# Quantising the feed-forward's weights inside the second attention's loop instead of in the quantised attention's preparation

## The chip, the cores and the metric

The kernel is one program on one core of a Trainium2 chip. Its time is the device time of one execution in microseconds. The five engines run their own instruction streams and meet at semaphores: TensorE (PE, with its weight loads as PEld), VectorE (DVE), ScalarE (ACT), GpSimd (POOL) and SyncE (SP), whose queue issues nearly all DMAs.

## What is computed

A decoder of four layers over 16 tiles of 128 tokens with 256 features. Each layer adds a gated attention and a gated feed-forward to `x`:

```python
x = x + tanh(g_xattn[1]) * L1_xattn(layernorm(x), ctx)      # the second attention, 32 heads of 8
x = x + tanh(g_ffn[1])   * L1_ffn(layernorm(x))             # sparse mixture of experts
x = x + tanh(g_xattn[2]) * L2_xattn(layernorm(x), ctx)      # the quantised attention, 16 heads of 16
x = x + tanh(g_ffn[2])   * L2_ffn(layernorm(x))             # the quantised feed-forward
```

The change is about the weights of the last of these. They are quantised to integers of 4 bits, which depends on nothing but the weights themselves:

```python
def weight_scale(W):
    return max(abs(W)) / 7
sw1 = weight_scale(W1)                        # W1: 1024 x 256
W1_q = clip(round(W1 / sw1), -8, 7) * sw1
b1_q = clip(round(b1 / (s1 * sw1)), INT32_MIN, INT32_MAX) * (s1 * sw1)
# the same for W2 (256 x 1024), b2 and s2
```

## The kernel before

The program is a row of stages with a barrier between them. Three are named here. The order of the instructions on each engine is written out by hand, and every dependence is a semaphore that the code waits for.

**The second attention, `rms_attention`.** After projections (a block of its own) it has a loop over the 16 tiles `t`, 797 to 911 us in the profile. GpSimd prepares the queries and keys of a tile in `stacks(t)` (six or so short instructions, L1080 to L1088) and the values in `values_staged(t)` (L1091); it runs one tile ahead. TensorE transposes the queries (`queries_turned`, `rms_TT<-rms_qs`) and the keys (`keys_turned`, `rms_TT<-rms_ks`), multiplies them (`scores`, L1287), multiplies with the values (`values`, L1301) and turns the result back (`turned_back`, L1311). ScalarE copies the queries and takes the exponentials. VectorE has, for each tile, `output(t - 1, 1)`, `evacuate(t, 0)` (L1374), `keys(t + 1)` (L1367, the copy `rms_kT`), `output(t, 0)`, `evacuate(t, 1)` and the statistics for the next layer (L1391). SyncE issues nothing in this loop.

**The quantised attention's preparation, in `quantised_attention`,** 1265 to 1372 us: SyncE loads the context, the attention's weights, and last, in `next_weights.load`, the feed-forward's weights as float32 (`qf_f`, 1 MB each), its biases and scales. Then come the projection of keys (`keys(p)`, pairs of tiles), values with the transposes of the normalised rows (`rows_turned`, and `low(p)` on VectorE, L2317), the values' integers (`value_integers`, L2348 to L2355), the transposes of keys, values and queries (`qa_TR`), and the projection of queries (`queries(p)`). The main loop over 256 pairs of tile and head follows.

**Class `QuantisedWeights`** quantises the feed-forward's weights within that preparation. Its VectorE steps stand between the `low(p)` and between the `queries(p)`: `magnitudes` (greatest absolute value of each partition, L1963), `scales` (seven instructions on two columns, L1968 to L1976), `divided` (L1993), `integers` (L1997), `hidden_bias` (four instructions on 8 columns) and `output_bias` (three on 256 columns). `greatest` is one GpSimd instruction, which takes the maximum over the partitions:

```python
    def greatest(self, pool):
        pool.wait_ge(self.s_am, 2)
        self.nc.gpsimd.partition_all_reduce(self.amx[:, :], self.am[:, :], P, bass.bass_isa.ReduceOp.max).then_inc(self.s_amx, 1)
```

It stands between the last `key_halves` and the 16 additions of `qa_bp` to `X` (L2131). `chained` gives an instruction a semaphore and makes VectorE wait for it before the next.

Of the kernel before, what the change touches and what calls it, by code (L numbers as in the profile page):

```python
# [7 lines left out]
F32 = mybir.dt.float32  # L8
# [1038 lines left out]
def rms_attention(nc, sh, ctxT, weights, gate, clear):  # L1047
# [13 lines left out]
    with ExitStack() as ctx:  # L1061
# [188 lines left out]
        ROUNDS = NB * NR  # L1250

        with nc.Block() as block:
            @block.gpsimd
            def _(pool):
                for t in range(2, NB):
                    pool.wait_ge(s_TK, t - 1)
                    stacks(pool, t)
                    pool.wait_ge(s_O, 2 * (t - 1))
                    values_staged(t)
# [102 lines left out]
            def _(dve):  # L1362
# [33 lines left out]

                keys(0)
                for t in range(NB):
# [9 lines left out]
                    if t:  # L1408
                        next_statistics(t - 1)
                output(NB - 1, 1)  # L1410
# [502 lines left out]
class QuantisedWeights:  # L1913


    F, NF = 1024, 8

    def __init__(self, nc, ctx, a):
        self.nc, self.a = nc, a

        def sb(n, shape, dt=F32):
            return ctx.enter_context(nc.sbuf_tensor("qf_" + n, shape, dt))

        self.w1 = sb("w1", [P, KT * self.F], F16)
        self.w2 = sb("w2", [P, self.NF * D], F16)
        self.b1 = sb("b1", [P, self.NF])
        self.b2 = sb("b2", [P, D])
        self.sa = sb("sa", [P, 2])
        self.rsa = sb("rsa", [P, 2])
        self.c = sb("c", [P, 8])  # L1930

    def prepare(self, ctx):
        nc = self.nc

        def sb(n, shape, dt=F32):
            return ctx.enter_context(nc.sbuf_tensor("qf_" + n, shape, dt))

        self.f1 = sb("f1", [P, KT * self.F])
        self.f2 = sb("f2", [P, self.NF * D])
        self.am, self.amx, self.sw, self.rsw = (sb(x, [P, 2]) for x in ("am", "amx", "sw", "rsw"))  # L1940
        self.s_load, self.s_am, self.s_amx, self.s_c, self.s_w = (
            nc.alloc_semaphore(name="qf_" + n) for n in ("load", "am", "amx", "wchain", "weights"))

    def load(self, sp):
        a = self.a
        sp.dma_start(self.f1[:, :], a["qf_w1"]).then_inc(self.s_load, 16)
        sp.dma_start(self.f2[:, :], a["qf_w2"]).then_inc(self.s_load, 16)
        sp.dma_start(self.b1[:, :], a["qf_b1"]).then_inc(self.s_load, 16)
        sp.dma_start(self.b2[:, :], a["qf_b2"].partition_broadcast(P)).then_inc(self.s_load, 16)
# [7 lines left out]
    def start(self, dve):  # L1957
        self.chained = chain_on(dve, self.s_c)

# [1668 lines left out]
```

## Time and profile before

| | |
|---|---|
| median of 3 runs | 2326.14 us (2323.9 to 2328.3) |
| the profiled execution | 2327.31 us, span 2325.6 us |
| PE busy | 1923.0 us, 83% |
| DVE busy | 1656.2 us, 71% |
| ACT busy | 1343.0 us, 58% |
| POOL busy | 896.6 us, 39% |
| granted TensorE clock, mean | 0.798 of full speed |

The shares are means over stages with different limits, so they don't say what a change in one stage is worth. For that the stage's own instructions are read in order of time: which instruction had to wait, and who released it. The clock in the profile's windows is a share of full speed: 1.00 is 2.4 GHz and 0.50 is 1.2 GHz.

### The profile page before, as it was taken

What the parts mean: (1) busy time and instruction counts of PE and PEld (TensorE: products, weight loads), DVE (VectorE), ACT (ScalarE), POOL (GpSimd) and SP (SyncE); (2) the same over time, 40 slices, a digit from 0 to 9 for tenths busy, and PEclk for the clock granted to TensorE, in tenths of its full rate; (3) what the DMA queues carried; (4) which work ended last, traced back from release to release, by engine and by line L of the source; (5) the groups of instructions that cost most, each with busy time, mean ns of one, the idle gap of its engine ahead of it and who ended that gap; (6) DMA issues with size and microseconds to landing.
All of it is one profiled execution on the core that took longest, in us unless ns stands there. A gap on an engine that the chain in (4) does not pass through costs nothing. (4 is left out here: it accounts for less than half of the span.)

```text
span 2325.6 us, 49109 instructions
## 1 busy us (share of the span) xinstructions
PE 1923.0 (83%) x17689; PEld 1096.0 (47%) x17713; DVE 1656.2 (71%) x2772; ACT 1343.0 (58%) x1831; POOL 896.6 (39%) x779
## 2 busy tenths in 40 slices
PE   3875999999997786799997868888888888468855
PEld 1343656656564465478874433333333333334523
DVE  4776765555555566853336989999999999467975
ACT  3444643333334676543333459999999999445565
POOL 4750000000001462600024438888888888423301
PEclk8776999999998898999998765555555555588989
DMA  7334212122122303522223016666665667120100
GB/s 209 87 124 170 68 65 69 67 66 68 63 67 86 105 3 117 222 49 69 65 64 107 34 28 111 113 112 112 110 113 111 113 110 112 25 73 2 21 20 28
DMA packets 384868, 195.32 MB, mean 84 GB/s; under 512 B 312301, under 2 KB 355311, under 8 KB 382703
## 3 DMA queue, kind: packets, MB, share of 16 engines
q1 hardware_dynamic: 381617, 184.47, 32.8%
q0 software_dynamic: 3072, 8.39, 1.1%
q8 instruction: 120, 1.97, 0.4%
q14 instruction: 59, 0.48, 0.1%
HBM read 94.99 MB, written 23.09 MB: 51 GB/s over the span
## 5 line engine op out<-in xcount | busy, mean ns | idle before, releaser
L2470 POOL CAST qa_pT<-qa_eT 128x2048 bf16<-128x2048 uint8 x256 | 478.0, 1896 | 109.9 <-PE qa_OY L2496 94.4
L2583 ACT ACTIVATE qa_e<-qa_scores,qa_nb 128x2048 uint8<-128x2048 f32 x256 | 510.4, 1994 | 4.2
L2593 DVE TENSOR_SCALAR_CACHE_REDUCE qa_scores<-qa_S,qa_sq 128x1024 f32<-128x1024 f32 (+1 forms) x256 | 456.0, 1830 | 4.2 <-PE qa_S L2488 3.3
L2488 PE MATMUL qa_S<-qa_kT,qa_qT 32*128 32x512 f16 x1024 | 373.2, 615 | 95.6 <-DVE qa_scores L2593 94.2
L1118 POOL MEMSET rms_nothing<- 128x512 f16 x1 | 0.5, 525 | 580.2 <-POOLq L3517 580.2
L2488 PEld LDWEIGHTS qa_S<-qa_kT,qa_qT 32*128 32x128 f16 x1024 | 64.8, 108 | 310.1 <-DVE qa_scores L2593 266.9
L975 PE MATMUL moe_G<-hT,moe_W 128*128 (+1 forms) x792 | 193.8, 381 | 7.0 <-DVE moe_zero L943 7.0
L984 PE MATMUL moe_O<-moe_W,moe_ap 128*128 (+1 forms) x1584 | 194.5, 273 | 4.1 <-DVE moe_ap L939 4.1
L915 ACT ACTIVATE moe_ap<-moe_a 128x512 f16<-128x512 f32 x132 | 83.0, 629 | 193.2 <-DVE moe_a L937 193.2
L975 PE MATMUL moe_U<-hT,moe_W 128*128 (+1 forms) x792 | 193.0, 380 | 0.0
L984 PEld LDWEIGHTS moe_O<-moe_W,moe_ap 128*128 128x128 f16 x1584 | 154.7, 98 | 50.4 <-DVE moe_ap L939 3.9
L2593 DVE TENSOR_SCALAR_CACHE_REDUCE qa_scores<-qa_S,qa_sq,qa_first_mx 128x1024 f32<-128x1024 f32 x128 | 174.4, 1363 | 0.0
L2496 PEld LDWEIGHTS qa_OY<-qa_V,qa_pT 128*128 128x128 bf16 x4096 | 119.1, 104 | 111.0 <-POOL qa_pT L2470 68.1
L934 DVE TENSOR_TENSOR moe_t<-moe_sg,moe_wb 128x512 f32<-128x512 f32 x132 | 91.4, 692 | 112.1 <-ACT moe_sg L910 107.6
L939 DVE TENSOR_TENSOR moe_ap<-moe_a,moe_ap 128x512 f16<-128x512 f32 x132 | 91.5, 693 | 91.7 <-ACT moe_ap L915 91.7
L910 ACT ACTIVATE moe_sg<-moe_G 128x512 f32<-128x512 f32 x132 | 78.8, 597 | 132.9 <-PE moe_G L975 132.7
L2496 PE MATMUL qa_OY<-qa_V,qa_pT 128*128 128x16 bf16 x4096 | 130.7, 175 | 6.9 <-ACT qa_y L2568 4.1
L1807 PE MATMUL moe_GU<-moe_xs,moe_W 128*128 128x256 f16 x1104 | 129.5, 274 | 3.9 <-issue 3.9
L1723 DVE TENSOR_TENSOR moe_a<-moe_GU,moe_sg 128x512 f32<-128x512 f32 x78 | 53.8, 689 | 99.6 <-PE moe_GU L1807 87.6
L975 PEld LDWEIGHTS moe_U<-hT,moe_W 128*128 (+1 forms) x792 | 77.7, 98 | 94.1 <-issue 1.1
L1603 ACT ACTIVATE moe_ap<-moe_a 128x512 f16<-128x512 f32 x78 | 49.2, 630 | 119.1 <-DVE moe_a L1723 119.1
L1556 POOL DMA_INDIRECT H<-moe_ys_rows,moe_slot x32 | 31.5, 985 | 223.1 <-DMA moe_ys_rows<-moe_ys 213.6
(436 smaller groups left out, 3533.4 us busy)
## 6 DMA issues: line engine op xcount, KB each, us to landing
moe_wb<-weights_T SPq DMA_DIRECT2D x264, 128.0 KB, 2.8
moe_W<-in_moe_w SPq DMA_DIRECT2D x40, 384.0 KB, 11.5
moe_W<-in_moe_w SPq DMA_DIRECT2D x11, 1152.0 KB, 17.2
moe_xs_rows<-rms_nothing SPq DMA_DIRECT2D x46, 128.0 KB, 1.9
moe_ys_rows<-moe_ys SPq DMA_DIRECT2D x23, 256.0 KB, 2.1
conv_rows<-conv_parts SPq DMA_DIRECT2D x16, 256.0 KB, 3.2
qa_eT<-qa_e SPq DMA_TRANSPOSE x256, 3.1
conv_qst<-conv_rows SPq DMA_DIRECT2D x96, 32.0 KB
```

The source lines that it names most:

```text
L910: nc.scalar.activation(sg[:, u, :], G[:, u, :], ACT.Silu).then_inc(s_sg[u], 1)
L915: nc.scalar.activation(ap[:, u, 0, :], a[:, u, :], ACT.Copy).then_inc(s_hi[u], 1)
L934: nc.vector.tensor_tensor(t1[:, u, :], sg[:, u, :], wb[:, u, :], ALU.mult).then_inc(s_t1[u], 1)
L939: nc.vector.tensor_tensor(ap[:, u, 1, :], a[:, u, :], ap[:, u, 0, :], ALU.subtract).then_inc(s_lo[u], 1)
L975: last = nc.tensor.matmul(X_[:, u, :], sh.W[:, f, wp, base + k * P:base + (k + 1) * P], sh.hT[:, xp, k, bass.ds(c * CT, CT)], start=i == 0 ...
L984: last = nc.tensor.matmul(O[:, t, :], ap[:, u, xp, t * P:(t + 1) * P], sh.W[:, f, wp, 4 * P:TW], start=False, stop=False, skip_group_check ...
L1807: last = nc.tensor.matmul(out[:, half * SLOT_TILE:(half + 1) * SLOT_TILE], W[:, bass.ds(f, 1), wp, base + k * P:base + (k + 1) * P], xs[:, ...
L2470: nc.gpsimd.tensor_copy(pT[:, u % RING, :, :].rearrange("p (b r) q -> p b r q", r=2), pairs).then_inc(s_cast, 1)
L2488: last = nc.tensor.matmul(S[:, banks[i], :], qT[rows, g, t * P:(t + 1) * P], kT[rows, g, parts[i] * QW:(parts[i] + 1) * QW], start=True, s ...
L2496: last = nc.tensor.matmul(O[:, h * HD:(h + 1) * HD], pT[:, u % RING, b, :], V[:, b, h * HD:(h + 1) * HD], start=b == 0, stop=b == NB - 1)
L2583: nc.scalar.activation(e8[:, u % RING, :], scores[:, u % RING, :], ACT.Exp, bias=nb[:, p % 2, i:i + 1], accum_out=sums[:, u:u + 1]).then_i ...
L2593: nc.vector.tensor_scalar(target, S[:, banks[0]:banks[-1] + 1, :], sq[:, t, h:h + 1], so_far, ALU.mult, ALU.max, accum_out=greatest).then_ ...
```

## The change

All work on the feed-forward's weights and biases moves from the quantised attention's preparation into the second attention's loop. The float32 weights are loaded when the loop starts, VectorE quantises them in nine places at the end of an iteration, SyncE stores the results in DRAM, and the preparation only loads them from there (0.5 MB each, float16, and 274 columns of constants). The arithmetic is the same. New are a memset of the constants, which the loads wait for, three stores and their waits on SyncE's queue, and the three loads.

```diff
-def rms_attention(nc, sh, ctxT, weights, gate, clear):
+def rms_attention(nc, sh, ctxT, weights, gate, clear, staged, staged_gate):
...
+        staged.prepare(ctx)
 
         with nc.Block() as block:
+            @block.sync
+            def _(sp):
+                staged.load(sp)
+                staged.store(sp)
+
             @block.gpsimd
             def _(pool):
                 for t in range(2, NB):
+                    if t == 7:
+                        staged.greatest(pool)
                     pool.wait_ge(s_TK, t - 1)
                     stacks(pool, t)
                     pool.wait_ge(s_O, 2 * (t - 1))
                     values_staged(t)
...
+                staged.start(dve)
                 keys(0)
                 for t in range(NB):
...
                     if t:
                         next_statistics(t - 1)
+                    if t in (2, 3):
+                        staged.magnitudes(dve, t - 2)
+                    if t == 7:
+                        staged.scales(dve, staged_gate)
+                    if t in (8, 10):
+                        staged.divided(dve, (t - 8) // 2)
+                    if t in (9, 11):
+                        staged.integers(dve, (t - 9) // 2)
+                    if t == 12:
+                        staged.hidden_bias(dve)
+                    if t == 13:
+                        staged.output_bias(dve)
...
     def load(self, sp):
         a = self.a
+        sp.wait_ge(self.s_c, 1)
         sp.dma_start(self.f1[:, :], a["qf_w1"]).then_inc(self.s_load, 16)
...
+    def store(self, sp):
+        sp.wait_ge(self.s_w, 1)
+        sp.dma_start(self.home1, self.q1[:, :]).then_inc(self.s_home, 16)
+        sp.wait_ge(self.s_w, 2)
+        sp.dma_start(self.home2, self.q2[:, :]).then_inc(self.s_home, 16)
+        sp.wait_ge(self.s_b, 1)
+        sp.dma_start(self.home_constants, self.constants[:, :]).then_inc(self.s_home, 16)
+        sp.wait_ge(self.s_home, 48)
...
     def start(self, dve):
         self.chained = chain_on(dve, self.s_c)
+        self.chained(self.nc.vector.memset(self.constants[:, :], 0.0))
...
+    def load(self, sp):
+        sp.dma_start(self.w1[:, :], self.staged.home1).then_inc(self.s_load, 16)
+        sp.dma_start(self.w2[:, :], self.staged.home2).then_inc(self.s_load, 16)
+        sp.dma_start(self.constants[:, :], self.staged.home_constants).then_inc(self.s_load, 16)
+        sp.wait_ge(self.s_load, 48)
...
                     for p in range(PAIRS):
                         key_halves(p)
-                    next_weights.greatest(pool)
                     pool.wait_ge(s_norm, NB)
...
-                    next_weights.start(dve)
                     low(0)
-                    next_weights.magnitudes(dve, 0)
                     low(1)
-                    next_weights.magnitudes(dve, 1)
                     low(2)
...
                     low(3)
-                    next_weights.scales(dve, next_gate)
                     low(4)
-                    next_weights.divided(dve, 0)
                     low(5)
-                    next_weights.integers(dve, 0)
-                    next_weights.hidden_bias(dve)
                     low(6)
-                    next_weights.output_bias(dve)
                     low(7)
                     value_integers()
...
                     for p in range(PAIRS):
                         queries(p)
-                        if p == 3:
-                            next_weights.divided(dve, 1)
-                        if p == 5:
-                            next_weights.integers(dve, 1)
```

Three places show what the built program makes of it. First GpSimd's instructions in the second attention's loop, between tiles 6 and 7 (`rms_vx` ends tile 6, `rms_qkv` starts the stacks of tile 7). Before:

```order
L1087 TENSOR_TENSOR rms_qs<-rms_qkv,rms_qs 128x32x8
L1088 TENSOR_TENSOR rms_ks<-rms_qkv,rms_ks 128x32x8
L1091 COPY rms_vx<-rms_qkv 128x32x8
L1080 TENSOR_TENSOR rms_qkv<-rms_qkv,rms_rs 128x512
L1084 CAST rms_qs<-rms_qkv 128x32x8 x2
```

and now:

```order
L1087 TENSOR_TENSOR rms_qs<-rms_qkv,rms_qs 128x32x8
L1088 TENSOR_TENSOR rms_ks<-rms_qkv,rms_ks 128x32x8
L1091 COPY rms_vx<-rms_qkv 128x32x8
L1988 ISA
L1988 ISA staged_amx<-staged_am 128x2
L1080 ISA
L1080 TENSOR_TENSOR rms_qkv<-rms_qkv,rms_rs 128x512
L1084 CAST rms_qs<-rms_qkv 128x32x8 x2
```

The maximum over the partitions (`staged_amx`) comes with one unnamed instruction ahead of it and one behind it, which the builder adds; they stood around it in the preparation too (as `MODIFY_POOL_CONFIG` in the profile), and now all three stand ahead of tile 7's stacks.

Second VectorE's instructions at the end of iteration 7 of that loop, as they are now; the seven rows with `staged` are new, and each iteration from 8 to 13 has its own insertion in the same place:

```order
L1382 COPY rms_oT<-rms_O 128x512
L1403 BN_AGGR row_mv<-row_stats 128x2
L1399 BN_STATS row_stats<-X 128x6
L2002 RECIPROCAL staged_constants<-staged_sa 128x2
L2004 TENSOR_SCALAR staged_sw<-staged_amx 128x2
L2005 RECIPROCAL staged_rsw<-staged_sw 128x2
L2007 TENSOR_TENSOR staged_constants<-staged_sa,staged_sw 128x2
L2008 RECIPROCAL staged_constants<-staged_constants 128x2
L2009 TENSOR_TENSOR staged_constants<-staged_constants 128x1
L2010 TENSOR_TENSOR staged_constants<-staged_constants,gates 128x1
L1388 RECIPROCAL rms_inv<-rms_B 128x16
```

The insertion is behind the last statistics of an iteration and ahead of the first `output` of the next one, which has `evacuate` and the copy of the keys behind it.

Third VectorE's instructions in the quantised attention's preparation between two `low` steps (`hT<-qa_hT_TP`), before:

```order
L2317 TENSOR_TENSOR hT<-qa_hT_TP,hT 128x2x256
L1963 TENSOR_REDUCE qf_am<-qf_f 128x1
L2317 TENSOR_TENSOR hT<-qa_hT_TP,hT 128x2x256
L1963 TENSOR_REDUCE qf_am<-qf_f 128x1
L2317 TENSOR_TENSOR hT<-qa_hT_TP,hT 128x2x256
L2368 TENSOR_SCALAR qa_bp<-qa_bp,gates 128x256
```

and now:

```order
L2374 TENSOR_TENSOR hT<-qa_hT_TP,hT 128x2x256 x3
L2422 TENSOR_SCALAR qa_bp<-qa_bp,gates 128x256
L2374 TENSOR_TENSOR hT<-qa_hT_TP,hT 128x2x256 x5
```

The `low` steps stand next to each other, with only the scaling of `qa_bp` left among them.

## Rows read from the trace of the kernel before

**Rows 1.** windows by stage: span, each engine's busy us (instructions), PEclk, DMA share, GB/s

```profile
797.00:911.00 114.00, 93.30 (x1918) 69.42 (x1916) 67.22 (x176) 78.24 (x82) 59.15 (x113) 0.96 0.01 2
...
1265.00:1372.00 107.00, 80.01 (x501) 44.46 (x502) 81.50 (x136) 47.75 (x77) 50.52 (x51) 0.73 0.15 52
```

**Rows 2.** timeline, VectorE in the loop: start, us, instruction, [idle before <-releaser]

```profile
823.81 0.40 DVE L1391 BATCH_NORM_STATS2 row_stats<-X 128x6 f32<-128x256 f32 x1
824.56 0.26 DVE L1380 RECIPROCAL rms_inv<-rms_B 128x16 f32<-128x16 f32 x1 [0.35 <-PE rms_B L1311]
...
825.92 0.69 DVE L1374 COPY rms_oT<-rms_O 128x512 f32<-128x512 f32 x1 [0.40 <-PE rms_O L1301]
826.53 0.68 DVE L1367 COPY rms_kT<-rms_TT 128x1024 f16<-128x1024 f16 x1
```

**Rows 3.** timeline, TensorE in the loop, one tile apart

```profile
820.73 0.40 PE L1287 MATMUL rms_S<-rms_qT,rms_kT 32*128 32x128 f16 x8 [0.86 <-DVE rms_kT L1367]
...
823.31 0.62 PE L1265 MATMUL rms_TT<-identh,rms_qs 128*128 128x128 f16 x8
...
827.27 0.40 PE L1287 MATMUL rms_S<-rms_qT,rms_kT 32*128 32x128 f16 x8 [0.86 <-DVE rms_kT L1367]
```

**Rows 4.** timeline, GpSimd in the loop

```profile
820.30 0.67 POOL L1088 TENSOR_TENSOR rms_ks<-rms_qkv,rms_ks 128x256 f16<-128x256 f32 x1
823.14 0.40 POOL L1091 COPY rms_vx<-rms_qkv 128x256 f32<-128x256 f32 x1 [2.18 <-PE rms_O L1301]
823.50 1.08 POOL L1080 TENSOR_TENSOR rms_qkv<-rms_qkv,rms_rs 128x512 f32<-128x512 f32 x1
```

**Rows 5.** timeline, GpSimd in the quantised attention's preparation

```profile
1320.36 0.37 POOL L1955 PARTITION_ALL_REDUCE qf_amx<-qf_am  x1 [5.84 <-DVE qa_bp L2368]
1327.63 15.19 POOL L2131 TENSOR_TENSOR X<-X,qa_bp 128x256 f32<-128x256 f32 x16 [6.90 <-issue]
```

**Rows 6.** instructions of lines L1955 and L2131 on GpSimd's queue

```profile
L1955 POOLq MODIFY_POOL_CONFIG  x2: 15/15/15, 1314.5 to 1314.5; - x2
...
L2131 POOLq MODIFY_POOL_CONFIG  x2: 82/82/83, 1320.7 to 1320.7; - x2
```

**Rows 7.** windows at the loop's start and inside it, columns as in Rows 1

```profile
795.90:806.10 10.20, 6.50 (x88) 4.77 (x88) 0.93 (x2) 6.45 (x7) 3.81 (x7) 0.50 0.01 2
...
815.00:880.00 65.00, 56.40 (x1199) 42.22 (x1198) 41.77 (x109) 47.58 (x50) 42.24 (x80) 1.00 0.01 3
```

**Rows 8.** timeline, TensorE, 32 value products at either clock

```profile
804.33 1.89 PE L1301 MATMUL rms_O<-rms_E,rms_vx 128*32 128x128 f32 x32
...
808.88 1.08 PE L1301 MATMUL rms_O<-rms_E,rms_vx 128*32 128x128 f32 x32
```

**Rows 9.** VectorE on `qf_f` alone, then on `qf_b` alone; and `scales`, one line

```profile
1313.00:1330.00 17.00, 7.04 (x4) 1.00 0.01 1
1355.00:1364.00 9.00, 2.50 (x2) 1.00 0.01 2
...
1313.00:1330.00 17.00, 2.73 (x7) 1.00 0.01 1
...
L1970 DVE TENSOR_SCALAR qf_sw<-qf_amx 128x2 f32<-128x2 f32 x1 | 0.2, 170 | 0.5 <-POOL qf_amx L1955 0.5
```

**Rows 10.** instructions of line L2323: min/median/max ns

```profile
L2323 DVE TENSOR_SCALAR qa_sk<-qa_sk x8: 181/730/3712, 1280.2 to 1309.1; 128x32 f32<-128x32 f32 x8
```

**Rows 11.** timeline, TensorE in the preparation, its waits

```profile
1319.58 0.63 PE L2182 MATMUL qa_hT_TP<-ident,H 128*128 128x128 f32 x4 [0.87 <-DVE hT L2317]
...
1340.84 0.62 PE L2204 MATMUL qa_TR<-identh,qa_ints 128*128 128x128 f16 x8 [2.59 <-DVE qa_ints L2355]
...
1369.12 0.97 PE L2188 MATMUL qa_TR<-identh,qa_stack 128*128 128x128 f16 x8 [2.17 <-POOL qa_stack L2134]
```

**Rows 12.** timeline, ScalarE in the preparation

```profile
1330.22 9.65 ACT L2267 ACTIVATE qa_kT<-qa_TR 128x512 f16<-128x512 f16 x16 [4.04 <-PE qa_TR L2188]
```

**Rows 13.** DMA issues: count, KB each, median us to landing

```profile
qf_f<-in_qf_w SPq DMA_DIRECT2D x2, 1024.0 KB, 8.8
```

More of the change, by code:

```diff
@@ L1910, in tensor, with __init__, dram @@
                 last.then_inc(self.s_T, 1)
-class QuantisedWeights:
+class StagedWeights:
     F, NF = 1024, 8
-    def __init__(self, nc, ctx, a):
+    CONSTANTS = 8 + D + 8 + 2
+    def __init__(self, nc, a):
         self.nc, self.a = nc, a
[L1921 to L1930, printed above, removed]
+        def dram(n, width, dt):
+            return nc.dram_tensor("qf_home_" + n, [P, width], dt, kind="Internal").ap()
+        self.home1, self.home2 = dram("w1", KT * self.F, F16), dram("w2", self.NF * D, F16)
+        self.home_constants = dram("constants", self.CONSTANTS, F32)
     def prepare(self, ctx):
@@ L1988, in output_bias @@
         chained(nc.vector.tensor_scalar(b[:, :], b[:, :], MAGIC, 2.0 ** 31 - 1, ALU.subtract, ALU.min))
-        chained(nc.vector.tensor_scalar(b[:, :], b[:, :], -2.0 ** 31, None, ALU.max))
+        nc.vector.tensor_scalar(b[:, :], b[:, :], -2.0 ** 31, None, ALU.max).then_inc(self.s_b, 1)
     def divided(self, dve, i):
@@ L1995, in integers, with __init__, sb, quantised_attention @@
     def integers(self, dve, i):
-        f, w = (self.f1, self.f2)[i], (self.w1, self.w2)[i]
+        f, w = (self.f1, self.f2)[i], (self.q1, self.q2)[i]
         self.nc.vector.tensor_scalar(w[:, :], f[:, :], MAGIC, None, ALU.subtract).then_inc(self.s_w, 1)
-def quantised_attention(nc, sh, a, gate, next_weights, next_gate):
+class QuantisedWeights:
+    F, NF = StagedWeights.F, StagedWeights.NF
+    def __init__(self, nc, ctx, staged):
+        self.nc, self.staged = nc, staged
+        def sb(n, shape, dt=F32):
+            return ctx.enter_context(nc.sbuf_tensor("qf_" + n, shape, dt))
+        self.w1 = sb("w1", [P, KT * self.F], F16)
+        self.w2 = sb("w2", [P, self.NF * D], F16)
+        self.constants = sb("constants", [P, staged.CONSTANTS])
+        self.b1, self.b2 = self.constants[:, 0:8], self.constants[:, 8:8 + D]
+        self.c, self.rsa = self.constants[:, 8 + D:16 + D], self.constants[:, 16 + D:18 + D]
+        self.s_load = nc.alloc_semaphore(name="qf_load")
+    def load(self, sp):
[3 more added lines that the diff above has]
+        sp.wait_ge(self.s_load, 48)
+def quantised_attention(nc, sh, a, gate, next_weights):
     NH, HD = 16, 16
@@ L2041, in quantised_attention @@
             rsv = sb("rsv", [P, KT], F32, inner)
-            next_weights.prepare(inner)
             vT = cf
@@ L3539, in program @@
             mixture(MOE0, 0)
+        staged = StagedWeights(nc, a)
         with own_semaphores(nc):
-            rms_attention(nc, sh, a["ctxT"], {"q": a["rms_wq"], "kv": a["rms_wkv"]}, sh.gates[:, 2:3], xs_rows)
+            rms_attention(nc, sh, a["ctxT"], {"q": a["rms_wq"], "kv": a["rms_wkv"]}, sh.gates[:, 2:3], xs_rows, staged, sh.gates[:, 5:6])
         with own_semaphores(nc):
@@ L3544, in program @@
         with own_semaphores(nc):
-            quantised = QuantisedWeights(nc, ctx, a)
-            quantised_attention(nc, sh, a, sh.gates[:, 4:5], quantised, sh.gates[:, 5:6])
+            quantised = QuantisedWeights(nc, ctx, staged)
+            quantised_attention(nc, sh, a, sh.gates[:, 4:5], quantised)
         with own_semaphores(nc):
```

16 lines of the change are left out of this document (11 added, 5 removed).

## Prediction

> **What bounds the kernel now.** I read first the windows by stage [rows 1], for how busy each engine is in the two stages that the change touches; then the timeline of each engine in them, for who waits for whom. In the second attention's loop no engine is full: of the 114 us TensorE is busy 93, ScalarE 78, VectorE 67, GpSimd 59. It is a ring that takes 6.54 us a tile (820.73 to 827.27 for the same instruction [rows 3]). In each turn TensorE stops once, for 0.86 us, for VectorE's copy of the turned keys `rms_kT` [rows 3]. That copy starts the moment `evacuate` ends (825.92, then 826.53), and in front of it VectorE was idle only twice in that part of the turn: 0.35 us before `output(t, 1)` and 0.40 us before `evacuate` [rows 2]. So VectorE has 0.75 us to spare at the place of the insertions, and no more; its mean idle share (41%) lies elsewhere in the turn. GpSimd ends its stacks at 820.97 (820.30 + 0.67 [rows 4]), and TensorE takes them at 823.31 [rows 3]: 2.34 us to spare.
>
> In the preparation VectorE looks full (81.5 of 107 us [rows 1]), and the moved work seems to be what fills it. But other engines run close behind, as the gain below shows.
>
> **What the preparation gives back.** Removed from VectorE are 7.04 us on `qf_f` and 2.73 us on the biases between 1313 and 1330, 2.50 us between 1355 and 1364, and seven small instructions of some 0.2 us [rows 9]: 7.04 + 2.73 + 2.50 + 1.4 = 13.7 us. Of this little comes back.
> - First part. Without it `value_integers` starts about 3.9 us earlier (the `low` steps then follow ScalarE's copies), its product `qa_ints` too. TensorE waits for `qa_ints` at 1340.84 [rows 11]. But it also needs TensorE's key transposes copied out, and ScalarE does that in 16 copies back to back from 1330.22 to 1339.87 [rows 12]. So 0.97 us is free at once. TensorE's one stop for a `low` step, 0.87 us at 1319.58 [rows 11], goes as well and starts those copies by that much or a little more earlier: together 1.9 us.
> - Second part. The two `qf_f` instructions among the queries, 2.50 us, push VectorE's last queries back. TensorE, with its own projections and transposes, takes 2.6 us a pair there against VectorE's 2.4, an estimate from following the queries through the trace, so VectorE can't be ahead of it by all of that: 1.5 us comes back at the end, where TensorE waits 2.17 us (1369.12 [rows 11]).
>
> Sum: -3.4 us. The bounds are -1.9 (the first part alone) and -7 (TensorE's clock, half from about 1342 to 1352, stays full). The loads there shrink from 2 MB to 1.1 MB and were last on the queue anyway: nothing. GpSimd's additions of `qa_bp` start earlier; nobody waits for them.
>
> **What the loop pays for GpSimd.** The maximum over the partitions itself takes 0.37 us [rows 5]. On either side of it stands a `MODIFY_POOL_CONFIG`. From the first, at 1314.5 [rows 6], to the maximum at 1320.36, GpSimd is idle for 5.84 us; from the second, at 1320.7 [rows 6], to its next instruction at 1327.63 it is idle for 6.90 us [rows 5], and the profile names no one that it waits for there. Part of the first interval is a wait for VectorE: the second `magnitudes` was ready at about 1318.8. So the first switch costs between 1.5 and 5.84 us; as the second is 6.90 with nothing to wait for, I take 5.84 as a full switch. In the preparation both were covered, since nobody needed GpSimd. In the loop all three stand directly behind `rms_vx`, where GpSimd goes on without a pause (823.14 + 0.40, then 823.50 [rows 4]); its idle 2.18 us is ahead of `rms_vx` and covers nothing. Tile 7's stacks are 5.84 + 0.37 + 6.90 = 13.1 us late, and behind them wait `queries_turned(7)` on TensorE, which blocks everything after it there, then ScalarE and VectorE. Less the 2.34 to spare: **+10.8 us**. Bounds: 8.8 - 2.3 = 6.5 with the short first switch, 11.8 with two at 6.90.
>
> The Trainium skill (GPSIMD Engine Reference, 2.1 Instruction dispatch) says that the first call of a freshly loaded kernel pays about 6 us, measured as the gap from the configuration to that call less the wait. Taken so, two switches give 5.95 x 2 + 0.37 - 2.34 = 9.9 us, an estimate by that page; our first interval less its wait is 1.5 us, so here loading and waiting overlapped, and only the second agrees.
>
> **The clock behind that stop.** After the pause before the loop, TensorE's granted clock was 0.50 from 795.9 to 806.1 and 1.00 after [rows 7]; TensorE restarted at about 796.6. A pause of 11 us should do the same. At half clock 32 value products take 1.89 us against 1.08 [rows 8], 1.75 times. TensorE's 5.67 us a tile (56.40 / 65 x 6.54 [rows 7]) would be 9.9 if all of it stretched so, and about 9 if two thirds do; in the 9.5 us at half clock that is about one tile, **+3.2 us**. Bounds 0 (no drop) and 4.3.
>
> **What the loop pays for VectorE.** Nine insertions, t = 2, 3 and 7 to 13. The same instructions took 13.7 us. Each has 0.75 us to spare and passes the rest on: `rms_kT` is later by it, TensorE stands still, and the ring has no slack in which to catch up. 13.7 - 9 x 0.75 = 6.9 us. The largest are the two reductions, 2.2 us each, so 1.45 each.
>
> Besides, the insertion starts at 824.21, when GpSimd's `rms_qkv` runs to 824.58 [rows 2, 4]. A VectorE instruction on SBUF alone that meets GpSimd can be held: L2323, on 32 columns, took 181 ns at best, 730 in the median and 3712 once, when GpSimd had three instructions in a row [rows 10]. With 0.37 us for each of the seven insertions that have a `TENSOR_SCALAR`: +2.6 us. **+9.5 us** together. Bounds: 6.9 without any wait; if each of the seven waits to the end of GpSimd's stacks, at 827.5, it is 7 x 3.3 = 23 instead of 2.6, so 30.
>
> The Trainium skill (SBUF — State Buffer, Who interferes with whom) has GpSimd and VectorE lock each other out of a shared pair of ports, whole instructions long, with `tensor_scalar` among those that take it and `tensor_reduce` never. By that rule the two reductions pay nothing extra and the others 0.37 us or more, which is what the sum has; the trace shows the holding, not whether a lock is handed over in the short gaps of the stacks.
>
> **Hidden.** The loads, 1 MB in 8.8 us [rows 13], are issued before the first keys and needed at t = 2, more than 20 us later. The memset falls in VectorE's wait before the first key copy. The stores (0.5 MB twice) start behind t = 9, 11 and 13, and the last, of 0.14 MB, has two tiles, 13 us, until the block's end; if that cover were gone it would be some 3 us. Nothing else is on SyncE's queue in the loop.
>
> **Sum.** -3.4 + 10.8 + 3.2 + 9.5 = +20.1 us. The profiled execution took 2327.31 us with its span of 2325.6, so 1.7 us lies around the span, and it is 1.2 us above the median of 2326.1. Neither changes with the edit: the profiled one would be 2347.4, the median 2346.2. I predict **2346 us, slower by 0.86%**.
>
> **Rivals.**
> - *The insertions are free*: VectorE is idle 41% of the loop, and TensorE might catch up. Then -3.4 + 10.8 + 3.2 gives 2337. Against it: the 0.86 us for `rms_kT` in each turn. Chance 0.11.
> - *The first switch is short or overlaps*, the 1.5 us of its lower bound: 4.3 less, 2342. For it speaks that the maximum began 1.5 us after its input. 0.13.
> - *Port waits run long*: VectorE is held through two or three of GpSimd's instructions per insertion, some 1.9 us instead of 0.37, so +10: 2356. For it the one wait of 3.7 us, against it the median. 0.13.
> - *The switch costs nothing in the loop* (the other side): if GpSimd's idle time around the maximum was something of the preparation and not of the switch, the stop at t = 7 is 0.37 us and hidden, and the clock does not drop. Place: GpSimd between `rms_vx` of tile 6 and the stacks of tile 7; price: the 14.0 us of both terms. With insertions at their 6.9 us that is -3.4 + 6.9, 2330, within 0.2% of before. It decides when the stop is under 2.34 us plus about one. Against it the 6.90 us with nothing to wait for. 0.06, and 0.02 for an actual gain through more from the preparation.
> - *As forecast*: 0.55, with its own range 2340 to 2353.
>
> **How the numbers follow.** Where this kernel's measurement can tell a change from none is about 0.2%, 4.7 us: faster is below 2321.4, slower above 2330.8. All but the fourth rival are slower: faster 0.02, same 0.06, slower 0.92. The range 2335 to 2358 takes in the free insertions at the bottom and the long port waits at the top; it leaves out the fourth rival and the far ends, less than 2 in 10.
>
> **What would show it.** In the loop: GpSimd idle for 5 to 7 us on either side of the maximum; TensorE waiting some 11 us for the stacks of tile 7 with the clock at 0.50 after it; `rms_kT` waits of 0.86 us grown to about 2.3 at two tiles and to 1.3 to 2 at seven more; the stage from 797 to 911 longer by 23 to 24 us. In the preparation: `qa_ints` ahead of ScalarE's last key copy, the stage 3 to 4 us shorter. The prediction is wrong if the stop of GpSimd is below 6 us, if `rms_kT` is not late, or if insertions wait for GpSimd's whole burst.

## The result, and the profile after

The changed kernel takes 2346.1 us in the median of six runs, against 2325.0 us in six runs of the kernel before, measured beside it. The ratio is 1.0083, with a 95% interval of 1.0064 to 1.0101, so the change makes the kernel slower by 15 to 23 us.

The two profiled executions alone would mislead: their spans are 2325.6 and 2332.9 us, 7.3 us apart, and the changed kernel's, of 2334.6 us, is 11.5 us below its median. The stages tell why. Windows by stage of the changed kernel (span, busy us and instructions of PE, PEld, DVE, ACT, POOL, then PEclk, DMA share, GB/s): all before the loop, the loop from the first `rms_TT` to the mixture's first instruction, the projection of keys, values with `rows_turned`, and the transposes and queries:

```profile
0.00:790.30 790.30, 679.29 (x5081) 400.09 (x5082) 474.34 (x783) 323.44 (x519) 126.08 (x88) 0.94 0.29 97
790.30:928.20 137.90, 100.17 (x1920) 74.55 (x1920) 81.35 (x198) 78.63 (x82) 62.85 (x115) 0.88 0.07 27
...
1283.40:1318.70 35.30, 24.14 (x129) 11.86 (x130) 22.02 (x47) 12.05 (x20) 23.25 (x22) 0.66 0.38 128
1318.70:1338.10 19.40, 18.35 (x115) 10.82 (x113) 13.20 (x20) 12.96 (x24) 14.16 (x20) 1.00 0.00 1
1338.10:1379.20 41.10, 31.80 (x258) 21.19 (x256) 27.07 (x50) 22.87 (x33) 6.51 (x10) 0.72 0.00 1
```

The same windows of the kernel before, by its own landmarks:

```profile
0.00:796.60 796.60, 687.30 (x5080) 402.63 (x5081) 475.22 (x782) 323.75 (x519) 126.22 (x88) 0.92 0.30 96
...
796.60:911.20 114.60, 93.69 (x1920) 69.82 (x1920) 67.33 (x177) 78.44 (x82) 59.35 (x114) 0.96 0.01 2
1266.20:1308.20 42.00, 30.73 (x129) 13.87 (x130) 27.47 (x50) 12.05 (x20) 24.16 (x22) 0.51 0.38 132
1308.20:1329.60 21.40, 20.07 (x114) 11.28 (x113) 19.63 (x34) 12.97 (x24) 5.88 (x8) 0.93 0.00 1
1329.60:1371.50 41.90, 28.71 (x261) 19.08 (x260) 34.35 (x53) 22.70 (x33) 20.46 (x22) 0.85 0.00 1
```

The loop is longer by 23.3 us, 137.9 against 114.6. Two stages with the same TensorE instructions are shorter: all before the loop by 6.3 us (granted clock 0.94 against 0.92) and the projection of keys by 6.7 us (0.66 against 0.51). The last two stages are 2.0 and 0.8 us shorter. Whether the 6.7 us belongs to the change is the first question for the experiments.

In the loop, the timeline of GpSimd shows the maximum with its two switches, which answers to [rows 5]:

```profile
834.07 0.40 POOL L1091 COPY rms_vx<-rms_qkv 128x256 f32<-128x256 f32 x1 [3.82 <-PE rms_O L1309]
840.05 0.38 POOL L1988 PARTITION_ALL_REDUCE staged_amx<-staged_am  x1 [5.58 <-issue]
847.24 1.06 POOL L1080 TENSOR_TENSOR rms_qkv<-rms_qkv,rms_rs 128x512 f32<-128x512 f32 x1 [6.82 <-issue]
```

GpSimd is idle 5.58 us ahead of the maximum, with its input ready since tile 3, and 6.82 us behind it. TensorE in the same place, against [rows 3]:

```profile
822.49 0.40 PE L1295 MATMUL rms_S<-rms_qT,rms_kT 32*128 32x128 f16 x8 [2.43 <-DVE rms_kT L1375]
...
831.65 0.40 PE L1295 MATMUL rms_S<-rms_qT,rms_kT 32*128 32x128 f16 x8 [2.12 <-DVE rms_kT L1375]
...
838.20 0.40 PE L1295 MATMUL rms_S<-rms_qT,rms_kT 32*128 32x128 f16 x8 [0.86 <-DVE rms_kT L1375]
...
851.24 1.03 PE L1273 MATMUL rms_TT<-identh,rms_qs 128*128 128x128 f16 x8 [10.39 <-POOL rms_ks L1088]
...
857.28 0.60 PE L1295 MATMUL rms_S<-rms_qT,rms_kT 32*128 32x128 f16 x8 [0.79 <-DVE rms_kT L1375]
...
888.15 0.40 PE L1295 MATMUL rms_S<-rms_qT,rms_kT 32*128 32x128 f16 x8 [1.59 <-DVE rms_kT L1375]
```

TensorE waits 10.39 us for the stacks of tile 7. Its 0.86 us for `rms_kT` grew to 2.43 and 2.12 behind the two reductions and to 1.59 behind an integer step. The reader can take the loop apart by the distance of one tile's first scores to the next, which is 6.54 us in [rows 3], and 6.54 or 6.55 us in every turn of the kernel before but the first. What exceeds 6.54 is: 1.58 and 2.62 us behind the reductions of t = 2 and 3, 12.54 and, in the next turn, 1.66 around the stop, 0.95 behind `scales`, 1.37, 0.73, 0.73 and 0.74 behind the four big steps, 0.42 behind `hidden_bias`, nothing behind `output_bias`. Their sum is 23.3, the whole growth of the loop. (In the turn behind the first big step the excess is 1.37 and the wait 0.86: a drop of the clock, below, took the place of the wait.)

Three of these have a part that the waits don't show. Windows of TensorE (busy us, PEclk):

```profile
823.50:826.90 3.40, 3.40 (x54) 0.50 0.00 0
...
844.00:861.00 17.00, 8.98 (x112) 0.50 0.00 1
...
874.70:878.10 3.40, 3.40 (x46) 0.50 0.00 0
```

The clock is at half (1.2 GHz) from 844, inside the stop, until 861, 9.8 us after TensorE restarts; that is the 3.8 us in the two steps around the stop beyond the wait of 10.39. And it falls to half for 3.4 us twice more, at 823.5 and 874.7, where TensorE had only waited for late key copies. These two drops make 2.62 and 1.37 of what would be 1.58 and 0.73.

### The profile page after: what moved, and what is told of

Same layout as the page of the kernel before. It is cut to its first block and busy times, and to the rows that moved or that the text cites. A ratio compares the mean times of both kernels' runs of the same rounds, so it can differ in the third digit from the quotient of the medians.

```text
span 2332.9 us, 49118 instructions
## 1 busy us (share of the span) xinstructions
PE 1914.2 (82%) x17689; PEld 1097.0 (47%) x17713; DVE 1650.0 (71%) x2773; ACT 1343.0 (58%) x1831; POOL 892.6 (38%) x779
## 5 line engine op out<-in xcount | busy, mean ns | idle before, releaser
L1828 PEld LDWEIGHTS moe_GU<-moe_xs,moe_W 128*128 x1104 | 108.8, 99 | 17.5 <-issue 4.2
```

What stands on the lines that cost most here:

```text
L1828: last = nc.tensor.matmul(out[:, half * SLOT_TILE:(half + 1) * SLOT_TILE], W[:, bass.ds(f, 1), wp, base + k * P:base + (k + 1) * P], xs[:, ...
```

## The experiments

### The changed kernel once more

No edit.

> The changed kernel once more, unaltered, for a second profile. Forecast: the same terms, so 2344 to 2348 us, 20 us over the kernel before; loop stage 137 to 138 us (first rms_TT to the first instruction of the mixture), with the stop of 10 to 11 us for GpSimd and TensorE at half clock behind it. One question is open here: in the first profile of the changed kernel the projection of keys in the quantised attention took 35.3 us where it took 42.0 before, with 24 us at half clock instead of 44. If the change causes that (ScalarE, VectorE or the queue act otherwise there), it comes again, 35 us; if it is chance of the execution, this profile can show anything from 35 to 42.

Measured: 2347.9 us, ratio 1.0111 (1.0081 to 1.0141), which overlaps with the first interval. Windows of this profile, the loop and the preparation's three stages:

```profile
791.50:928.20 136.70, 98.54 (x1920) 73.70 (x1920) 81.30 (x198) 78.54 (x82) 62.87 (x115) 0.90 0.08 27
1283.10:1325.10 42.00, 30.74 (x129) 13.74 (x130) 27.45 (x50) 12.08 (x20) 24.16 (x22) 0.51 0.32 107
1325.10:1345.30 20.20, 20.06 (x114) 11.34 (x113) 12.61 (x17) 12.75 (x24) 13.09 (x19) 0.93 0.00 1
1345.30:1383.80 38.50, 27.95 (x258) 18.84 (x255) 27.05 (x50) 22.56 (x33) 6.72 (x11) 0.85 0.00 1
```

The projection of keys takes 42.0 us at clock 0.51, as before the change. So the 6.7 us were chance of one execution, and the question is settled by the same program. At the clock of the kernel before (0.93 and 0.85 in the last two stages of both) these stages are 1.2 and 3.4 us shorter: the preparation gives back 4.6 us here, and 2.8 us in the first profile, whose last stage ran at 0.72. The stop was 10.36 us again (TensorE restarts at 853.17), but the clock behind it came back 3.9 us after the restart and not 9.8:

```profile
847.20:857.10 9.90, 3.93 (x52) 0.50 0.01 2
```

The step around the stop exceeds 6.54 by 12.05 us and the next one by nothing, so the clock cost 1.7 us and not 3.8. Two short drops of the clock came here as well, behind the second reduction and behind the first big step.

### The maximum through DRAM instead of GpSimd

```diff
-                    if t == 7:
-                        staged.greatest(pool)
...
+    def turn(self, sp):
+        sp.wait_ge(self.s_am, 2)
+        sp.dma_start(self.am_home, self.am[:, :]).then_inc(self.s_amd, 16)
+        sp.wait_ge(self.s_amd, 16)
+        sp.dma_start(self.amb[:, :, :], self.am_home.rearrange("p i -> (p i)").partition_broadcast(P)).then_inc(self.s_amb, 16)
...
+        chained(nc.vector.tensor_reduce(out=self.amx[:, :], in_=self.amb[:, :, :].rearrange("p q i -> p i q"), axis=AXX, op=ALU.max))
```

> The changed kernel with the maximum over partitions taken without GpSimd: SyncE stores the 128x2 maxima in DRAM and loads them back to every partition, VectorE reduces 128x2x128 at the head of the scales of tile 7. No switch on GpSimd; all else, insertions too, as in the changed kernel. Theory (switch 10.8 to 10.4 of stop and 3.2 to 3.8 of clock): 14 us less than the changed kernel, about 2332, less 0.4 us for the longer scales; loop stage 124. Rival 'the switch costs nothing, the insertions do it all': no change, 2346. Rival 'insertions are free': 2346 - 20 = 2326 or so. The round trip of the maxima has four tiles, 26 us, and should be hidden; if it is not, the wait is at the scales of tile 7.

Measured: 2332.0 us, ratio 1.0028 (1.0013 to 1.0044), loop 125.2 us. Windows of the loop and of the preparation's last two stages together; then SyncE's queue at the round trip:

```profile
793.00:918.20 125.20, 96.86 (x1920) 72.14 (x1920) 82.03 (x199) 78.55 (x82) 62.67 (x114) 0.92 0.10 31
1315.40:1375.40 60.00, 49.16 (x370) 30.26 (x368) 39.64 (x66) 35.64 (x57) 19.82 (x28) 0.87 0.00 1
```

```profile
831.35 0.33 SPq L1990 DMA_DIRECT2D staged_am_home<-staged_am  x1
834.27 0.33 SPq L1992 DMA_DIRECT2D staged_amb<-staged_am_home  x1
```

The store is done after 2.9 us (the second transfer is issued then), and nobody waits for the round trip. Its price is VectorE's reduction of 0.42 us at the head of `scales`: that turn exceeds 6.54 by 1.59 us instead of 0.95. Without GpSimd's part the loop is 12.7 and 11.5 us shorter than in the two profiles of the changed kernel, and 10.6 us longer than before; 2.0 us of that are two short drops of the clock to half. Both rivals fall: the switch costs, and the insertions cost.

### The switch alone, in the kernel before

```diff
+                nc.gpsimd.memset(spare[:, :], 1.0).then_inc(s_spare, 1)
+                pool.wait_ge(s_spare, 1)
                 for t in range(2, NB):
+                    if t == 7:
+                        nc.gpsimd.partition_all_reduce(spare[:, 2:4], spare[:, 0:2], P, bass.bass_isa.ReduceOp.max).then_inc(s_spare, 1)
```

> The kernel before, with one addition: GpSimd takes an idle maximum over partitions of a 128x2 tile of ones ahead of the stacks of tile 7 in the second attention's loop; nobody reads it. Nothing of the quantisation is moved. Theory: both switches and their clock fall on the path, 10.4 to 10.8 + 3.2 to 3.8 = 13.6 to 14.6 us more than before, about 2340. Rival 'the switch costs nothing in the loop': 2326. Rival 'first switch short when nothing is waited for' (1.5 us): 2335.

Measured: 2337.3 us, ratio 1.0066 (1.0043 to 1.0089), loop 127.0 us, +12.4. GpSimd and TensorE in its timeline:

```profile
838.57 0.37 POOL L1261 PARTITION_ALL_REDUCE rms_spare<-rms_spare  x1 [5.78 <-issue]
845.80 1.06 POOL L1080 TENSOR_TENSOR rms_qkv<-rms_qkv,rms_rs 128x512 f32<-128x512 f32 x1 [6.86 <-issue]
```

```profile
836.52 0.40 PE L1293 MATMUL rms_S<-rms_qT,rms_kT 32*128 32x128 f16 x8 [0.86 <-DVE rms_kT L1373]
849.79 1.03 PE L1271 MATMUL rms_TT<-identh,rms_qs 128*128 128x128 f16 x8 [10.63 <-POOL rms_ks L1088]
855.33 0.40 PE L1293 MATMUL rms_S<-rms_qT,rms_kT 32*128 32x128 f16 x8 [0.87 <-DVE rms_kT L1373]
```

With none of VectorE's insertions in the loop and an input that was ready before tile 2, the first switch is 5.78 us. That rules out the rival of a short first switch (1.5 us). The stop is 10.63 us; the step from 836.52 to 855.33 is 18.81, that is 12.27 over 6.54, so the clock costs 1.6 us; it came back 3.8 us after TensorE's restart. The total, +15 us (10 to 21), agrees with this but is less sharp. The two single parts add up in the loop: 12.4 us for the switch and 10.6 us for the insertions are 23.0, against 23.3 and 22.1 for both in one kernel.

### No quantisation at all

Three memsets ahead of the first key copy fill what is stored in the homes; the loads, GpSimd's `greatest` and VectorE's nine insertions are left out, so the last feed-forward computes with empty weights:

```diff
-                staged.load(sp)
                 staged.store(sp)
...
-                    if t in (2, 3):
-                        staged.magnitudes(dve, t - 2)
...
-                    if t == 13:
-                        staged.output_bias(dve)
```

> The changed kernel without the quantisation: no loads of the float32 weights, no VectorE or GpSimd work on them; the homes in DRAM are filled with zeros and ones from three memsets before the loop, so the last feed-forward computes with empty weights (that part of the computation is left out). It measures what the preparation alone gives back. Theory: loop as before, 114.6 us; preparation -3.4 us by the forecast (bounds -1.9 and -7), total about 2322.7. If the shorter projection of keys of the changed kernel's profile (-6.7 us) is caused by the change and not by chance, total about 2316.

Measured: 2322.0 us, ratio 1.0000 (0.998 to 1.0021).

```profile
791.90:906.60 114.70, 93.75 (x1920) 69.88 (x1920) 69.32 (x180) 78.45 (x82) 59.26 (x114) 0.96 0.04 13
1301.90:1359.60 57.70, 47.01 (x373) 30.27 (x373) 40.17 (x68) 35.59 (x57) 19.81 (x28) 0.87 0.00 1
```

The loop is that of before, and values, transposes and queries take 57.7 us where the kernel before has 21.4 + 41.9 = 63.3, 5.6 us less at about the same clock (0.93 and 0.85 before, 0.87 here). The interval of the total reaches from -4.6 to +4.9 us and so just holds a gain of 4; it shows that the time taken away, 13.7 us of VectorE, isn't given back, and rules out the 9.5 us by which the first profile's preparation seemed shorter.

### TensorE kept busy through the stop

```diff
                 def queries_turned(t):
+                    if t == 7:
+                        pe.wait_ge(s_kT, t)
+                        for i in range(160):
+                            nc.tensor.transpose(TT[:, i % NG, :], sh.identh[:, :], sh.identh[:, :])
                     pe.wait_ge(s_lo, t + 1)
-                    if t:
+                    if t and t != 7:
                         pe.wait_ge(s_kT, t)
```

> The changed kernel with 160 idle transposes of the identity into the free rms_TT on TensorE ahead of its wait for the stacks of tile 7, so that TensorE stays busy through GpSimd's stop. The stop itself remains. Theory: the half clock behind the stop (from 844 to 861 us in the changed kernel) is due to TensorE's pause; without the pause the steps behind it are at full clock and the kernel is 3.8 us faster than the changed one, 2342. Rival 'the half clock there has another cause, or costs nothing': 2346.

Measured: 2340.3 us, ratio 1.0073 (1.0052 to 1.0094), loop 136.4 us. TensorE in its timeline, then two windows, through the stop and behind it:

```profile
841.48 9.11 PE L1280 MATMUL rms_TT<-identh 128*128 128x128 f16 x160
852.09 0.62 PE L1273 MATMUL rms_TT<-identh,rms_qs 128*128 128x128 f16 x8 [1.51 <-POOL rms_ks L1088]
```

```profile
841.50:850.60 9.10, 9.09 (x162) 1.00 0.01 2
850.60:867.70 17.10, 13.89 (x296) 1.00 0.01 3
```

The clock stays at 1.00 and the step around the stop exceeds 6.54 by 10.47 us, against 14.20 (in two steps), 12.05 and 12.27 without filling. So the half clock behind the stop is due to TensorE's pause and costs 1.6 to 3.7 us: the mechanism is shown, and the gain of 3.8 us that I expected is the top of it. The loop won only 0.3 to 1.5 us, because three dips of the clock to half, of 3.4 us each, fell elsewhere in it (two in the changed kernel). The total, 0.1% under the changed kernel's first ratio and 0.4% under its second, doesn't tell 1.6 from 3.8.

### The insertions at another place

The kernel with the maximum through DRAM; the nine `if t ...` lines stand ahead of `output(t, 0)`:

```diff
                     if t + 1 < NB:
                         keys(t + 1)
+                    if t in (2, 3):
+                        staged.magnitudes(dve, t - 2)
...
+                    if t == 13:
+                        staged.output_bias(dve)
                     output(t, 0)
                     evacuate(t, 1)
```

> The kernel with the maxima through DRAM, with its nine insertions whole as they were, but at another place of the iteration: behind the copy of the turned keys and ahead of output(t, 0), where VectorE is idle for 1.08 us, and further on for 0.39, 0.35 and 0.40 us before the next key copy. Theory (only what VectorE has to spare ahead of the next key copy counts): 2.2 us to spare there instead of 0.75, so that of the insertions (2.27 us twice, 1.54 us four times, 2.0, 1.4 and 0.9 us) next to nothing passes on; loop 115 to 116 us, total about 2320 to 2322, 10 us less than with the maxima through DRAM and the old places. Rival 'TensorE waits for output(t, 0) or evacuate(t, 1) instead': what exceeds 1.08 us passes on, 1.19 x 2 + 0.46 x 4 + 0.9 + 0.3 = 5.4 us, loop 120, total 2326.

Measured: 2332.1 us against 2337.2 for the kernel before, measured beside it (on another chip than the runs above: a stage that no edit touches, the mixture, takes 368 us there instead of 355), ratio 0.999 (0.9974 to 1.0007). Window of the loop; VectorE at t = 2; TensorE in the two turns with the reductions:

```profile
791.10:907.10 116.00, 93.89 (x1920) 69.82 (x1920) 80.78 (x199) 78.42 (x82) 59.57 (x114) 0.96 0.10 33
```

```profile
814.59 0.68 DVE L1374 COPY rms_kT<-rms_TT 128x1024 f16<-128x1024 f16 x1
815.19 2.28 DVE L2001 TENSOR_REDUCE staged_am<-staged_f 128x1 f32<-128x2048 f32 x1
...
819.69 0.26 DVE L1387 RECIPROCAL rms_inv<-rms_B 128x16 f32<-128x16 f32 x1 [0.35 <-PE rms_B L1318]
```

```profile
819.00 0.66 PE L1318 MATMUL rms_B<-ident,rms_oT 128*128 128x128 f32 x4 [0.47 <-DVE rms_oT L1381]
```

The loop is 116.0 us instead of 125.2. At t = 2 the reduction takes 2.28 us, and VectorE has caught up when it waits 0.35 us again before `output(t, 1)`, so the next key copy is on time. The theory holds for `rms_kT`. The rival holds in small: at the two reductions TensorE stops 0.47 us for `rms_oT`, and these turns exceed 6.54 by 0.54 each; with 0.18 once more the insertions cost 1.3 us, where the old places cost 10.2 (8.2 of waits and the 2.0 of the clock).

### VectorE's work in pieces

Again without GpSimd's maximum. The reductions are cut to 512 columns, `divided` and `integers` to 1024, `scales` and the biases to one or two instructions, and `piece(t, 0)` stands behind `keys(t + 1)`, `piece(t, 1)` at the end of the iteration:

```diff
                         keys(t + 1)
+                    staged.piece(t, 0)
                     output(t, 0)
...
+                    staged.piece(t, 1)
...
+        self.pieces = {(1, 1): greatest_of(0), (2, 0): greatest_of(1), (2, 1): greatest_of(2), (3, 0): greatest_of(3),
...
+                       (8, 0): div(0, 0), (9, 0): div(0, 1), (10, 0): whole(0, 0), (11, 0): whole(0, 1),
```

> As the kernel with the maxima through DRAM, and VectorE's work cut to fit its idle time: reductions of 512 columns, divisions and integers of 1024 columns, scales and biases two instructions at a time, in two places of each iteration from tile 1 to 15: behind the copy of the turned keys (1.08 us idle there) and at the end (0.75 us). The same work, with more and shorter instructions. Theory (ring with 0.75 and 1.08 us to spare, port waits about 0.26 us each): next to nothing passes on, loop 115 to 117 us, so the preparation's gain remains: 2322 to 2325, that is 0 to 0.2% faster than before. Rival 'each VectorE instruction among GpSimd's pays the port': 27 pieces x 0.3 us or more = 8 us, 2331.

> The kernel with VectorE's work in pieces once more, unaltered, since its first interval (0.9962 to 1.0003) does not tell it from the kernel before. Theory: loop 115.0 and the preparation 3.4 to 4.6 us shorter, 0.15 to 0.2% faster than before; the stages from the first qa_VP to the first qa_S take 58.7 us at 10 us of half clock.

Measured: 2321.2 us against 2322.3, ratio 0.9983 (0.9962 to 1.0003); again, on the other chip, 2334.1 against 2337.2, 0.9995 (0.9979 to 1.001). The window of the loop in the first profile (115.4 us in the second), then one of VectorE's groups there:

```profile
799.40:914.40 115.00, 93.69 (x1920) 69.88 (x1920) 83.19 (x211) 78.46 (x82) 59.49 (x114) 0.96 0.11 33
```

```profile
L2026 DVE TENSOR_SCALAR staged_f<-staged_f,staged_rsw 128x1024 f32<-128x1024 f32 x4 | 3.7, 917 | 0.0
```

VectorE is busy 83 us of the loop instead of 67, and all turns are 6.54 or 6.55 us but the first, as before, and one of 6.74 (6.75 in the second profile). So 16 us more work in the loop cost 0.2 us in the turns, and 0.4 us in the loop as a whole: the rival of 8 us for the ports falls, since what VectorE waits for GpSimd there (0.74 to 1.00 us for one and the same kind of piece) is covered too. Neither interval tells this version from the kernel before, and the same is so of the insertions behind the key copy. By the stages it should be 4 us faster (0.4 us more in the loop, some 4.6 less in the preparation), 0.2% or about what can be measured; that it beats the kernel before is not shown.

### The kernel before once more

> The kernel before once more, unaltered, for a second profile and as a measure of the method: ratio 1.000. The projection of keys took 25.9 to 32.6 us in seven profiles with the same instructions; here it can be any of these. The stages from the first qa_VP to the first qa_S should take 63 us again (63.3 and 62.9 in the two profiles with the quantisation in the preparation, 57.6 to 60.5 in the six without).

Measured: 2339.2 against 2337.2 us, ratio 1.000 (0.9978 to 1.0022). Windows of the loop and of the preparation's last two stages, and the latter for the pieces, measured beside it:

```profile
793.60:908.60 115.00, 94.15 (x1920) 70.13 (x1920) 67.38 (x178) 78.48 (x82) 59.25 (x114) 0.95 0.01 2
1319.10:1384.80 65.70, 53.00 (x369) 32.25 (x368) 53.93 (x86) 35.92 (x57) 26.25 (x29) 0.79 0.00 1
```

```profile
1318.10:1380.30 62.20, 51.47 (x370) 32.32 (x368) 40.27 (x69) 35.83 (x57) 20.71 (x29) 0.81 0.00 1
```

The clock in these stages differs from one execution to the next whichever the kernel is, here 0.79. I expected 63 us and it took 65.7. The projection of keys, counted as in the expectation, from its own first matmul, took 32.6 us, the upper end of what was seen.

## Why the prediction was right

Forecast 2346 us and +20.1; measured 2346.1, and +19.3 by the ratio (15 to 23). The mechanisms were right; that the sum came out so near is in part luck, since two terms were off and an effect that was not forecast made up for it:

| term | forecast | measured |
|---|---|---|
| preparation gives back | -3.4 | -4.6 (mean of eight profiles less mean of three) |
| GpSimd's stop | +10.8 | +10.4, +10.4, +10.6 |
| the clock behind it | +3.2 | +3.8, +1.7, +1.6; gone when TensorE was kept busy |
| VectorE's insertions | +9.5 | +7.5, and 1.7 and 2.1 more for short dips of the clock |
| loop as a whole | +23.5 | +23.3, +22.1 |

**What bounds the loop.** Right: a ring without slack. What delays `rms_kT` beyond what VectorE has to spare ahead of it is never caught up, as every turn of 6.54 us behind a long one shows. It was shown from both sides: the same nine insertions cost 10.2 us with 0.75 us to spare and 1.3 us with 2.2 us to spare, and the same work in pieces 0.2 us.

**GpSimd's stop.** Right, in size and in the mechanism. The first switch was the open part, 1.5 to 5.84 us by [rows 5]; it is 5.50 to 5.78 us in the loop with its input long ready, and the second 6.82 to 7.14. The estimate of 9.9 us from the first-call figure of the Trainium skill (GPSIMD Engine Reference, 2.1 Instruction dispatch), taken for both switches, was as near as mine: 5.58 + 0.38 + 6.82 less the 2.34 to spare are 10.4, so 5.95 us are too much for the first switch and too little for the second. The 1.5 us in the preparation fit loading that overlaps with a wait: the time from the configuration to the maximum is nearly the same with a wait in it (5.84) and without (5.50 to 5.78).

**The clock behind the stop.** The mechanism is right, and keeping TensorE busy showed it. The size is that of one execution: half clock lasted 9.8 us after TensorE's restart in the first profile, 3.9 us in the second and 3.8 us with the switch alone, and 3.8, 1.7 and 1.6 us were paid. The forecast took 9.5 us at half clock from [rows 7] as if that were fixed. (In its working, two thirds of 5.67 us stretched 1.75 times give 8.5 us a tile and not 9; the 3.2 us come out with 8.5, as 9.5 / 8.5 x 2.8.)

**The insertions.** Their term, 9.5 us, was mis-sized: without the clock they cost 7.5. The two reductions passed on 1.58 each (forecast 1.45), the four big steps 0.73 each (forecast 0.5 and 0.37 for the port), `scales` 0.95 (1.0), and the two biases 0.42 and nothing, where the forecast had 2.0 for both. So `rms_kT` was late at five tiles behind the reductions and not at seven: nothing was left of the insertion at t = 13, and a drop of the clock hid that at t = 8. Two things were wrong with the port waits. The big steps took 1.54 us instead of 1.28 and 1.22, so 0.26 and 0.32 us each and not 0.37. And the 2.73 us of the biases held port waits already: two instructions took 0.83 and 0.70 us in the preparation, where GpSimd's additions had just begun (1327.63 in [rows 5]), and 0.29 each in the loop, where all seven took 2.13. This is the first of the two, in the kernel before:

```profile
L1988 DVE TENSOR_SCALAR qf_b<-qf_b 128x256 f32<-128x256 f32 x1 | 0.8, 829 | 0.0
```

This is the row of `divided` in the changed kernel, against 1.28 in the preparation before:

```profile
L2027 DVE TENSOR_SCALAR staged_f<-staged_f,staged_rsw 128x2048 f32<-128x2048 f32 x2 | 3.1, 1539 | 0.0
```

The reduction took 2.27 us in the loop and 2.28 in the preparation before (the forecast said 2.2), so it was not held, as the Trainium skill has it (SBUF — State Buffer, Who interferes with whom). But the residual addition behind it was: 0.68 us where it is 0.35 in the loop of before. Both its tensors lie in SBUF, and the insertion moved it to 829.72, beside GpSimd's `rms_ks` (829.58 to 830.25). That this is what held it is read from the rows and not tried by itself. The forecast had no such knock-on. It used up most of the 0.40 us that VectorE waits next and that was to cover part of the insertion; without it a reduction would have passed on some 1.25 us and not 1.58, an estimate from these rows. Timeline of VectorE behind the second reduction, then the same instruction in the kernel before:

```profile
829.72 0.68 DVE L1394 SCALAR_TENSOR_TENSOR X<-rms_on,gates,X 128x128 f32<-128x128 f32 x1
```

```profile
825.18 0.35 DVE L1386 SCALAR_TENSOR_TENSOR X<-rms_on,gates,X 128x128 f32<-128x128 f32 x1
```

What made up the 2 us that were missing wasn't in the forecast: two or three dips of the clock to half for 3.4 us, each behind turns in which TensorE had waited 1.6 to 2.4 us for key copies, at a price of 0.6 to 1.5 us each, 1.7 us in the first profile and 2.1 in the second. That they fill the gap is luck. They come in every version whose insertions make TensorE wait so and in none of the others (before, no quantisation, pieces, behind the key copy; the switch alone has only the drop at its stop). That the waits cause them is inferred from this, not tried by itself.

**The preparation.** The mechanism came as forecast: `qa_ints` ends at 1345.0 and TensorE waits for ScalarE's last key copy instead. Timeline of ScalarE, then TensorE, of the changed kernel's first profile, against [rows 11, 12]:

```profile
1338.73 9.95 ACT L2324 ACTIVATE qa_kT<-qa_TR 128x512 f16<-128x512 f16 x16 [4.03 <-PE qa_TR L2245]
```

```profile
1348.82 1.01 PE L2261 MATMUL qa_TR<-identh,qa_ints 128*128 128x128 f16 x8 [1.51 <-ACT qa_kT L2324]
...
1376.80 1.03 PE L2245 MATMUL qa_TR<-identh,qa_stack 128*128 128x128 f16 x8 [2.39 <-POOL qa_stack L2191]
```

The size was low. From the first `qa_VP` to the first `qa_S` it took 63.3, 62.9 and 65.7 us with the quantisation and 57.7 to 62.2 without; at like clock the difference is 4.6 us (0.93 and 0.85 in both kernels) or 3.5 (0.79 and 0.81). Set side by side at like clock, the second profile of the changed kernel is 2.0 us shorter up to the first `qa_ints` transpose, where the forecast's first part had 1.9, and 2.5 us shorter behind it. So the term that was mis-sized is the second part: 1.5 us in the forecast, 2.5 measured. The estimate that TensorE needs 2.6 us a pair against VectorE's 2.4 was right (the queries of the last pairs follow one another every 2.61 us in the second profile), but it was taken for a limit on what comes back; in the kernel before VectorE, with the two `qf_f` steps, was the late one, and all of the 2.5 us came back. The place was off by one as well: TensorE's last wait, 2.17 us in [rows 11], stayed (2.39), and the one ahead of it shrank from 1.70 to 0.20 us. Of the 13.7 us removed, 9 are still not seen again: they were beside other engines' work.

**Hidden.** The loads and stores cost nothing that a row shows: the float32 weights landed 5.8 us after their issue, and the turns up to the first reduction kept their 6.54 us.

**The rivals.** Free insertions: wrong, +10.6 us without any switch. A short first switch: wrong. Long port waits: wrong, some 0.3 us each. A switch that costs nothing: wrong, +12.4 us alone. (Its 2330 us also left out the 2.6 us of port waits without a reason.)

## What to carry to other kernels

In a ring that repeats every few microseconds an engine's idle share says nothing; what counts is what it is idle between the insertion and the next instruction on which the bounding engine waits. Read that off a timeline, and move or cut the insertion to fit: the same work cost 10.2, 1.3 or 0.2 us here. Don't put a GpSimd instruction that needs a switch of its configuration where another engine needs GpSimd within 13 us; here a round trip of 1 KB through DRAM, with four tiles of time, was hidden and cost only its reduction on VectorE. And compare kernels by stage and at like clock before reading a difference of two profiles: these two are 7.3 us apart in one execution each, and 19 us in the interval.

## What the runs showed of the hardware

- GpSimd's switch there and back around one `PARTITION_ALL_REDUCE` of 0.37 us costs 5.5 to 5.8 us ahead and 6.8 to 7.1 us behind, in four profiles of the loop. It is paid for the way back to ordinary instructions too.
- The granted clock of TensorE fell to 0.50 during a pause of 10.4 to 10.6 us and came back 9.8 us after the restart in one execution and 3.9 and 3.8 us after it in two others; that cost 3.8, 1.7 and 1.6 us. With 160 idle transposes in the pause it stayed at 1.00.
- The clock also fell to 0.50 for 3.4 us while TensorE was busy (3.40 us of 3.40), behind turns with waits of 1.6 to 2.4 us; that the waits are the cause is inferred.
- The projection of keys, the same instructions in all kernels, ran at 0.51 or 0.66 and took 42.0 or 35.3 us, with one and the same program.
- A `TENSOR_SCALAR` of 128x2048 took 1.54 us among GpSimd's short instructions in the loop and 1.28 us in the preparation, where GpSimd stood idle beside it; a `TENSOR_REDUCE` of the same size took 2.27 and 2.28.
